# Local attention of a second layer on one core: token tiles on TensorE's row groups, keys with 32 tokens of the tile ahead, one score matmul for four heads

## The chip, the cores and the metric

The kernel runs on one core of a Trainium2 chip (trn2). The metric is the device time of one execution in microseconds (us); less is better. The core has five engines that run side by side and meet only at semaphores: TensorE (PE: matmuls, whose weight loads are listed apart as PEld), VectorE (DVE), ScalarE (ACT), GpSimd (POOL) and SyncE (SP), which issues transfers.

## The reference

Four blocks act on a hidden state x of 2 sequences of 1024 tokens with 128 features: window attention with 16 heads, a Fourier layer, an attention block (a global and a local attention), again the Fourier layer, a location-weighted layer, a mixture of experts, ReLU attention with its feed-forward part, and again experts. The change is in the local attention, which works on RMS-normed x:

```python
def local_gqa_attn(x, wq, wk, wv, wo):        # 16 heads of 8 features, 4 key heads
    q = split_heads(x @ wq, H)
    k = split_heads(x @ wk, KVH)
    v = split_heads(x @ wv, KVH)
    q, k = (rope(q, BASE_L), rope(k, BASE_L))
    q, k = (qk_norm(q), qk_norm(k))
    k, v = (repeat_kv(k), repeat_kv(v))
    i = jnp.arange(x.shape[1])
    diff = i[:, None] - i[None, :]
    mask = (diff >= 0) & (diff < WIN)         # WIN = 32
    return merge_heads(sdpa(q, k, v, mask)) @ wo
```

`rope` turns pairs of features by an angle that depends on the position, `qk_norm` divides each head by its root mean square, `sdpa` is softmax attention. A query sees itself and the 31 tokens ahead of it.

## The kernel before, in words

All 2048 tokens stay in SBUF, features on the 128 partitions and tokens along the free axis, in four chunks of 512 (`NC`), two for each sequence. Everything is float32 here, and a float32 matmul shows as two records in the trace (and two weight loads). Each engine runs a list of instructions of its own, in the order in which the functions of the same name stand in its block (`@block.tensor`, `@block.scalar` and so on); no planner moves them. They wait for one another at semaphores that only count up (`q["sc"]` counts score units in PSUM, `q["ex"]` exponentials done, and so on; `WAS` holds the counts of the attentions before). The local attention is the third attention (`AL`), in three parts.

**Heads** (`normed_heads(AL)`, on PE at L1794, DVE L1283, ACT L907, POOL L693). It works in eight units, queries and keys of each chunk by turns. PE projects a chunk twice (plain and rotated weights, 128 rows and columns, 512 tokens), DVE multiplies by the rope table and adds (L1303, L1304, L1307), ACT squares (L912), PE sums over each head ("var"), ACT takes logarithm and exponential (L919, L922), and POOL multiplies the factor in (L700). After every second unit PE projects the values of a chunk (8 records with the tokens as weights) and ACT copies them (L929). Queries and keys then have the four heads of a group on four row groups of 32 partitions. PE issues the var matmul of a unit behind the projection of the next one.

**Attention** (`local_attention` on PE at L1912, `local_soft` on ACT at L967, `local_attention` on DVE at L1348). It runs over eight passes (2 sequences x 4 groups of heads), each in two halves of four tiles of 128 tokens: 16 steps n. In a step PE computes scores (`scores(n)`, L1916) into PSUM banks 0 to 3, one bank for each head, in two pairs of heads: 32 matmuls of 32 rows x 64 columns of the array, each 64 keys against 96 queries. ACT exponentiates each pair (L986), DVE multiplies by the band mask (L1363), and two steps later PE multiplies by the values (`values(n)`, L1938) with matmuls of 64 rows x 32 columns: per tile 384 and 256 wide for the two halves of the keys, and 128 wide for the queries of the next tile. A pair of scores waits for the exponential of the same pair one step before. DVE masks the keys of the group for one pass ahead (`group_keys`, L1316), and ACT and DVE copy the sums out after every second pass (L974, L976, L1357).

**End** (`attention_end`). Denominators, reciprocals, the division, the output projection (64 records of 32x128 for two chunks), and the residual sums.

SP loads the rope tables: the local one (1 MB) when the heads of the global attention no longer need theirs (L660).

## Time and profile before

| | |
|---|---|
| median of 3 runs | 1024.35 us (1015.62, 1024.35, 1024.69) |
| the profiled execution | 1023.21 us, its span 1021.1 us |
| PE, DVE, ACT, POOL busy | 948.7, 535.3, 540.0, 147.7 us |
| mean granted clock of TensorE | 0.948 of full |
| projections of the local attention start | at 367.7 us of the span |
| its first score matmul | at 396.37 us |
| its last value matmuls | at 454.55 us |

The span is what the profiler saw between the first and the last instruction. The "granted clock" is TensorE's clock as a share of 2.4 GHz; it has two levels, 1.00 and 0.50 (1.2 GHz), and a mean between them is a mixture. Matmuls in different parts of the array overlap, so a busy PE doesn't mean a full array.

### The profile page before, as it was taken

Reading aid. Unit: us, or ns where it says so; the run is one execution under the profiler, and the core shown is the slowest. Engines: PE = TensorE matmul, PEld = TensorE weight load, DVE = VectorE, ACT = ScalarE, POOL = GpSimd, SP = SyncE. Lnnn points to the kernel's source line nnn. Section 1 sums busy time; section 2 is a strip of 40 time slices with the busy share of each in tenths; the row PEclk is TensorE's granted clock in tenths of the full one; section 3 lists DMA queues with packets and bytes.
Section 4 is the critical chain, followed back from the end, with each engine's and each line's share of the span. In section 5 each row is a group of like instructions: output and inputs, shape, how many; then the busy total and the mean of one; then the engine's idle time right before and its main releaser. Section 6 shows DMA issues by size and latency. Waiting matters only on the chain.

```text
span 1021.1 us, 22819 instructions
## 1 busy us (share of the span) xinstructions
PE 948.7 (93%) x9990; PEld 436.0 (43%) x9990; DVE 535.3 (52%) x870; ACT 540.0 (53%) x767; POOL 147.7 (14%) x164
## 2 busy tenths in 40 slices
PE   7698978999999988988998999989999999999998
PEld 4476733433333335754443444434333333444443
DVE  4576545523324375665565525555666666423554
ACT  6044535889999856443765531256455454445121
POOL 3001120501001003120010120000223322004000
PEclk9899989899999997589998799999999999899999
DMA  7644050100000000000000057100000000001651
GB/s 205 215 128 125 7 218 0 42 2 2 2 2 2 2 1 1 3 3 2 0 1 0 1 135 138 62 1 1 2 2 2 2 2 2 0 1 43 160 123 52
DMA packets 16763, 43.16 MB, mean 42 GB/s; under 512 B 4844, under 2 KB 5292, under 8 KB 15244
## 3 DMA queue, kind: packets, MB, share of 16 engines
q1 hardware_dynamic: 15692, 39.51, 14.5%
q10 hardware_dynamic: 972, 2.20, 0.7%
q8 instruction: 79, 1.29, 0.5%
q14 instruction: 20, 0.16, 0.1%
HBM read 36.91 MB, written 4.55 MB: 41 GB/s over the span
## 4 chain that ended last, share of the span: by engine, by line
PE 82%; ACT 8%; DVE 6%; issue 2%; DMA 1%; POOL 1%; ACTq 0%; SPq 0%; DVEq 0%; POOLq 0%
PE ps L1639 82%; ACT nrr L816 1%; ACT nrr L818 1%; ACT nsq L809 1%; DVE mxq L1258 1%; ACT work L897 1%; POOL work L677 1%; ACT nrr L826 0%; ACT nrr L823 0%; DMA stf<-scr_k 0%; DVE aux L1451 0%; DVE work L1307 0%; DMA x<-in_x 0%; PE ps L2072 0%; DVE work L1363 0%
## 5 line engine op out<-in xcount | busy, mean ns | idle before, releaser
L1639 PE MATMUL ps<-rq,stf 32*64 32x512 f32 (+4 forms) x4096 | 208.4, 465 | 3.3 <-ACT hz L1001 1.6
L1639 PE MATMUL ps<-work,vbuf 64*32 64x128 f32 (+6 forms) x2992 | 195.5, 421 | 2.4 <-DVE nsq L1357 2.2
L1639 PE MATMUL ps<-hz,wsb 128*128 128x512 f32 (+1 forms) x352 | 161.9, 624 | 5.0 <-ACT nsq L842 2.5
L957 ACT ACTIVATE work<-ps 128x1024 f32<-128x1024 f32 x144 | 139.5, 1021 | 14.3 <-PE ps L1639 10.4
L1639 PEld LDWEIGHTS ps<-rq,stf 32*64 32x64 f32 x4096 | 97.5, 147 | 110.2 <-issue 84.1
L1019 ACT ACTIVATE work<-ps 128x1024 f32<-128x1024 f32 x72 | 73.6, 1024 | 75.7 <-PE ps L1639 75.7
L1639 PEld LDWEIGHTS ps<-work,vbuf 64*32 64x32 f32 (+1 forms) x2992 | 62.9, 111 | 116.1 <-issue 64.4
L1639 PEld LDWEIGHTS ps<-hz,wsb 128*128 128x128 f32 (+1 forms) x352 | 62.8, 192 | 85.3 <-issue 73.2
L1341 DVE TENSOR_TENSOR work<-work,csb 128x1024 f32<-128x1024 f32 (+1 forms) x40 | 40.7, 1018 | 97.2 <-ACT work L957 96.8
L1065 ACT ACTIVATE work<-ps 128x512 f32<-128x512 f32 x48 | 28.7, 597 | 117.2 <-PE ps L1639 117.2
L1639 PE MATMUL ps<-work,wsb 128*128 128x512 f32 (+1 forms) x176 | 87.0, 603 | 2.7 <-DVE work L1553 2.7
L1402 DVE TENSOR_SCALAR work<-ps 128x1024 f32<-128x1024 f32 (+3 forms) x72 | 68.5, 952 | 24.2 <-PE ps L1639 24.2
L897 ACT ACTIVATE work<-ps 128x512 f32<-128x512 f32 x64 | 37.4, 598 | 65.3 <-PE ps L1639 65.3
L1550 DVE TENSOR_TENSOR work<-ps,work 128x512 f32<-128x512 f32 x48 | 33.2, 691 | 64.0 <-ACT work L1065 40.8
L1639 PE MATMUL ps<-bsb 128*64 128x512 bf16 x256 | 53.1, 398 | 13.8 <-DMA stf<-scr_k 7.4
L1639 PE MATMUL ps<-nsq,csb 128*128 128x512 f32 (+3 forms) x152 | 53.3, 530 | 10.8 <-DVE nrr L1253 3.0
L809 ACT ACTIVATE nsq<-ps 128x512 f32<-128x512 f32 x40 | 23.5, 588 | 62.4 <-PE ps L1639 62.4
L1258 DVE TENSOR_REDUCE mxq<-ps 128x4 f32<-128x512 f32 x64 | 42.8, 688 | 22.3 <-PE ps L1639 21.3
L1639 PEld LDWEIGHTS ps<-work,wsb 128*128 128x128 f32 (+1 forms) x176 | 31.9, 189 | 50.0 <-issue 34.3
L738 POOL TENSOR_TENSOR work<-work,csb 128x512 f32<-128x512 f32 (+1 forms) x40 | 36.4, 911 | 106.7 <-ACT work L1019 106.7
L719 POOL TENSOR_SCALAR aux<-nsq,csb 128x1024 f32<-128x1024 f32 x8 | 24.2, 3025 | 156.8 <-DVE nsq L1328 110.4
L1639 PE MATMUL ps<-x,csb 128*128 128x512 f32 x64 | 35.6, 663 | 6.3 <-DMA x<-in_x 4.8
(200 smaller groups left out, 1172.9 us busy)
## 6 DMA issues: line engine op xcount, KB each, us to landing
stf<-scr_w SPq DMA_DIRECT2D x32, 256.0 KB, 4.5
stf<-scr_w SPq DMA_DIRECT2D x64, 128.0 KB, 3.3
stf<-scr_q SPq DMA_DIRECT2D x12, 192.0 KB
wsb<-in_w SPq DMA_DIRECT2D x1, 2192.0 KB, 12.5
rq<-in_rq SPq DMA_DIRECT2D x2, 1024.0 KB, 9.9
stf<-scr_k SPq DMA_DIRECT2D x9, 204.0 KB
rq<-scr_k SPq DMA_DIRECT2D x6, 204.0 KB
hz<-scr_k SPq DMA_DIRECT2D x6, 204.0 KB
```

Source lines behind the costliest of these rows:

```text
L719: nc.gpsimd.tensor_scalar(nums[:, b * S:(b + 1) * S], half_out[0][:, b * S:(b + 1) * S], c_("part")[:, 0:1], None, ALU.mult).then_inc(q["s ...
L738: nc.gpsimd.tensor_tensor(cells, cells, c_("keep").unsqueeze(1).unsqueeze(1) .broadcast_to(list(cells.shape)), ALU.mult).then_inc(q["mk"], 1)
L809: nc.scalar.activation(nsq[:, c], bank(c), ACT.Square).then_inc(n_sq, 1)
L897: nc.scalar.activation(prob[:, st, hd], bank(n % 2), ACT.Exp, scale=SCALE).then_inc(q["ex"], 1)
L957: nc.scalar.activation(probs_of(n)[:, 2 * k:2 * k + 2].rearrange("p h s -> p (h s)"), two(slot(2 * n + k)), ACT.Exp, scale=SCALE).then_inc ...
L1019: nc.scalar.activation(probs_of(n)[:, 0:2].rearrange("p h s -> p (h s)"), two(slot(2 * n)), ACT.Relu, scale=SCALE).then_inc(q["ex"], 1)
L1065: nc.scalar.activation(moe[:, 0, f % 2], bank(f % 2), ACT.Silu).then_inc(m_sg, 1)
L1258: nc.vector.tensor_reduce(mxq[:, k % 2, 4 * u:4 * u + 4], bank(4 + m % 2).rearrange("p (t s) -> p t s", t=4), AX.X, ALU.max).then_inc(w_m, 1)
L1341: nc.vector.tensor_tensor(cells, cells, c_("keep").unsqueeze(1).unsqueeze(1) .broadcast_to(list(cells.shape)), ALU.mult).then_inc(q["mk"], 1)
L1402: ins = nc.vector.tensor_scalar(to[:, :, lo:hi], src[:, :, lo:hi], SCALE, 0.0, ALU.mult, ALU.max)
L1550: nc.vector.tensor_tensor(product, bank(2 + f % 2), moe[:, 0, f % 2], ALU.mult).then_inc(m_su, 1)
L1639: return nc.tensor.matmul(o, l, r, start=start, stop=stop, skip_group_check=True)
```

## The change

Row groups stand for token tiles in place of heads. A query unit is one of the four heads of every group for all 2048 tokens: eight matmuls with 32 columns of weights each, every one for one tile of each chunk, write to four column groups (`queries`). There are four such units. Keys are computed for two chunks per unit and in 2 units, for each tile of 128 tokens with the 32 tokens ahead of it (`KW` = 160 columns); so there are 6 units and not 8. The values of a chunk follow each of the four query units. The first scores wait for all four query units. A score matmul has a tile's keys against the queries of four heads at once: in each of two pairs of tiles, two blocks of 32x64 that are 384 and 256 wide for each tile, and then, for both tiles, a block of 32x32 that is 128 wide and has the 32 keys ahead. The value matmuls are the eight of before (64x32, 384 and 256 wide), and then four of 32x32 in place of 64x32, 128 wide, for the 32 keys ahead. The exponentials, the masks and the copies out keep their sizes. The masked keys of the four groups are made once for both sequences, in 4 instructions of 640 columns in place of 2 of 512 and 7 of 1024. The second rope load becomes 0.33 MB. `normed_heads`, `rotated_consumed` and `group_keys` stay for the other attentions.

```diff
+KW = P + WIN_L
+UNITS_L = 2 + G
...
+        rope_l = rq[:, 0:4 * KW].rearrange("p (k c s) -> p k c s", k=2, c=CB)
+        q_l = qd[:, 0:T].rearrange("p (h s) -> p h s", h=G)
+        k_l = stf[:, NG * T - NC * KW:NG * T].rearrange("p (c s) -> p c s", c=NC)
+        kz_l = stf[:, 0:NG * NC * KW].rearrange("p (g c s) -> p g c s", g=NG, c=NC)
...
+            return CB * KW if m < 2 else CH
...
-            rope_load(1)
+            sp.dma_start(rope_l, rope_k.rearrange("k p c s -> p k c s")).then_inc(s_rope, 16)
...
+            def local_heads():
+                was = WAS[AL]
+                for m in range(UNITS_L):
+                    rt_ = rope_t[:, m % 4]
+                    pool.wait_ge(q["r"], was["r"] + m + 1)
+                    if m < 2:
+                        nc.gpsimd.tensor_tensor(k_l[:, CB * m:CB * (m + 1)].rearrange("p c s -> p (c s)"),
+                                                rt_[:, 0, 0:CB * KW], rt_[:, 2, 0:CB * KW], ALU.mult).then_inc(q["kn"], 1)
+                    else:
+                        nc.gpsimd.tensor_tensor(q_l[:, m - 2], rt_[:, 0], rt_[:, 2], ALU.mult).then_inc(q["q"], 1)
...
+            def local_heads():
+                was = WAS[AL]
+                for m in range(UNITS_L + 1):
+                    if m < UNITS_L:
+                        rt_, w = rope_t[:, m % 4], unit_width(m)
+                        act.wait_ge(q["rot"], was["rot"] + m + 1)
+                        nc.scalar.activation(rt_[:, 1, 0:w], rt_[:, 0, 0:w], ACT.Square).then_inc(q["sq"], 1)
+                    if m:
+                        rt_, w = rope_t[:, (m - 1) % 4], unit_width(m - 1)
+                        act.wait_ge(q["var"], was["var"] + m)
+                        if m > 4:
+                            act.wait_ge(q["kn"], was["kn"] + m - 4)
+                        nc.scalar.activation(rt_[:, 2, 0:w], bank(pair(AL, m - 1))[:, 0:w], ACT.Ln, bias=eps[:, 1:2])\
+                            .then_inc(q["ln"], 1)
+                        act.wait_ge(q["ln"], was["ln"] + m)
+                        nc.scalar.activation(rt_[:, 2, 0:w], rt_[:, 2, 0:w], ACT.Exp, scale=-0.5).then_inc(q["r"], 1)
+                    if 2 <= m < 2 + NC:
+                        c = m - 2
+                        act.wait_ge(q["v"], was["v"] + c + 1)
+                        act.wait_ge(s_vz, 6)
+                        for g in range(NG):
...
-                    rotated_consumed(AL, n)
...
+            def local_group_keys(g):
+                if g == 0:
+                    dve.wait_ge(q["kn"], WAS[AL]["kn"] + 2)
+                nc.vector.tensor_scalar(kz_l[:, g].rearrange("p c s -> p (c s)"), k_l.rearrange("p c s -> p (c s)"),
+                                        group_mask(g), None, ALU.mult).then_inc(q["kz"], 1)
+            def local_heads():
+                was = WAS[AL]
+                dve.wait_ge(s_rope, 32)
+                for m in range(UNITS_L):
+                    rt_, w, o = rope_t[:, m % 4], unit_width(m), pair(AL, m)
+                    dve.wait_ge(q["mm"], was["mm"] + m + 1)
+                    if m >= 4:
+                        dve.wait_ge(q["kn"], was["kn"] + m - 3)
+                    for i in range(2):
+                        if m < 2:
+                            to, src = rt_[:, i, 0:w], bank(o + i)[:, 0:w]
+                            turn = rope_l[:, i].rearrange("p c s -> p (c s)")
+                        else:
+                            to = rt_[:, i].rearrange("p (b c s) -> p b c s", b=B, c=CB)
+                            src = bank(o + i).rearrange("p (b c s) -> p b c s", b=B, c=CB)
+                            turn = rope_l[:, i, :, WIN_L:KW].unsqueeze(1).broadcast_to([P, B, CB, P])
+                        ins = nc.vector.tensor_tensor(to, src, turn, ALU.mult)
+                    ins.then_inc(q["t"], 1)
+                    dve.wait_ge(q["t"], was["t"] + m + 1)
+                    nc.vector.tensor_tensor(rt_[:, 0, 0:w], rt_[:, 0, 0:w], rt_[:, 1, 0:w], ALU.add)\
+                        .then_inc(q["rot"], 1)
+                    if m >= 4:
+                        local_group_keys(m - 4)
...
-                    if n % 2 == 0 and n // 2 + 1 < len(PASSES):
-                        group_keys(AL, *PASSES[n // 2 + 1])
+                    if n < 2:
+                        local_group_keys(2 + n)
...
+                by_row_group = z.rearrange("p (c j s) -> p j c s", c=NC, j=4)
+                def keys(m):
+                    for i in range(2):
+                        for j in range(4):
+                            for k in range(CB):
+                                at = (CB * m + k) * CH + j * P - WIN_L
+                                skip = max(0, -at)
+                                ins = mm(bank(pair(AL, m) + i)[32 * j:32 * j + 32, k * KW + skip:(k + 1) * KW],
+                                         wk[i][:, 0:32], z[:, at + skip:at + KW])
+                    ins.then_inc(q["mm"], 1)
+                def queries(m):
+                    hd = m - 2
+                    for i in range(2):
+                        for j in range(4):
+                            ins = mm(bank(pair(AL, m) + i)[32 * j:32 * j + 32].rearrange("p (c s) -> p c s", c=NC),
+                                     wq[i][:, 32 * hd:32 * hd + 32], by_row_group[:, j])
+                    ins.then_inc(q["mm"], 1)
+                for m in range(UNITS_L + 1):
+                    if m < UNITS_L:
+                        pe.wait_ge(n_z, normed(n, 2 * m + 1 if m < 2 else NC - 1))
+                        if m >= 3:
+                            pe.wait_ge(q["ln"], was["ln"] + m - 2)
+                        (keys if m < 2 else queries)(m)
+                    if 2 <= m < 2 + NC:
+                        v = m - 2
+                        if v >= 2:
+                            pe.wait_ge(q["vf"], was["vf"] + v - 1)
+                        values_by_token(v, bank(6 + v % 2), w_("l_wv")).then_inc(q["v"], 1)
+                    if m:
+                        pe.wait_ge(q["sq"], was["sq"] + m)
+                        mm(bank(pair(AL, m - 1))[:, 0:unit_width(m - 1)], c_("head"),
+                           rope_t[:, (m - 1) % 4, 1, 0:unit_width(m - 1)]).then_inc(q["var"], 1)
...
+                    c = CB * b + n % 2
+                    if n == 0:
+                        pe.wait_ge(q["q"], was["q"] + G)
                     if n % 2 == 0:
-                        pe.wait_ge(q["kz"], was["kz"] + keys_of(AL, n // 2))
+                        pe.wait_ge(q["kz"], was["kz"] + (NG if b else g + 1))
                     for pair in range(2):
                         u = 2 * n + pair
-                        if u < 2:
-                            pe.wait_ge(q["ln"], was["ln"] + 2 * NC - 2 + u)
-                        else:
+                        if u >= 2:
                             pe.wait_ge(q["ex"], was["ex"] + u - 1)
-                        for j in range(4):
-                            k0 = b * S + (4 * (n % 2) + j) * P
-                            for half in range(2):
-                                at = k0 + HB * half
-                                for hd in (2 * pair, 2 * pair + 1):
-                                    rows = slice(32 * hd, 32 * hd + 32)
-                                    ins = mm(bank(hd)[HB * half:HB * (half + 1), j * W_L:(j + 1) * W_L],
-                                             kz[rows, g, at:at + HB], qd[rows, at:at + W_L])
+                        def block(j, lo, m, q0, w):
+                            rows = slice(32 * j, 32 * j + 32)
+                            o = bank(j)[lo:lo + m, 0:G * W_L].rearrange("p (h s) -> p h s", h=G)
+                            at = HB if m == WIN_L else 0
+                            first = 0 if m == WIN_L else WIN_L + lo
+                            return mm(o[:, :, at:at + w], kz_l[rows, g, c, first:first + m],
+                                      q_l[rows, :, c * P + q0:c * P + q0 + w])
+                        for j in (2 * pair, 2 * pair + 1):
+                            block(j, 0, HB, 0, W_L)
+                            block(j, HB, HB, HB, HB)
+                        for j in (2 * pair, 2 * pair + 1):
+                            if (n % 2, j) != (0, 0):
+                                ins = block(j, P - WIN_L, WIN_L, 0, WIN_L)
                         ins.then_inc(q["sc"], 1)
...
                     for j in range(4):
-                        for half in range(2):
-                            rows = slice(HB * half, HB * (half + 1))
-                            lo, w = HB * half, min(W_L, P - HB * half)
-                            mm(by_tile(4 + 2 * half + st, j)[:, :, lo:lo + w],
-                               vq[rows, KT * b + 4 * st + j, g // 2, g % 2], heads[rows, :, j * W_L:j * W_L + w],
-                               opens and (half, st, j) != (1, 1, 0), False)
-                    rows = slice(HB, P)
-                    if opens and st == 0:
-                        mm(by_tile(6, 0)[:, :, 0:WIN_L], qd[rows, T:T + WIN_L], heads[rows, :, 0:WIN_L], False, False)
-                    for j in range(4 - st):
-                        lo = j * W_L + HB
-                        ins = mm(by_tile(7 if j == 3 else 6 + st, (j + 1) % 4)[:, :, 0:WIN_L],
-                                 vq[rows, KT * b + 4 * st + j, g // 2, g % 2], heads[rows, :, lo:lo + WIN_L],
-                                 opens and j == 3, False)
+                        block(j, 0, HB, 4 * st + j, 0, 0, W_L, opens)
+                        ins = block(j, HB, HB, 4 * st + j, HB, 0, HB, opens)
+                    for j in range(4):
+                        if st + j:
+                            ins = block(j, P - WIN_L, WIN_L, 4 * st + j - 1, 0, HB, WIN_L, False)
+                        elif opens:
+                            ins = block(j, P - WIN_L, WIN_L, -1, 0, 0, WIN_L, False)
                     ins.then_inc(q["pv"], 1)
...
+        for c in range(CB):
+            at = np.maximum(P * (4 * c + row // 32) - WIN_L + np.arange(KW), 0)
+            k[0, row, c] = cos_l[at, d // 2]
+            k[1, row, c] = sign * sin_l[at, d // 2]
```

## Rows read from the trace of the kernel before

**Rows 1.** The page: busy time of each engine.

```profile
PE 948.7 (93%) x9990; PEld 436.0 (43%) x9990; DVE 535.3 (52%) x870; ACT 540.0 (53%) x767; POOL 147.7 (14%) x164
```

**Rows 2.** Stretches: us, busy (x) of PE, PEld, DVE, ACT, POOL; granted clock; DMA.

```profile
391.78:395.19 3.41, 1.93 (x11) 1.35 (x10) 2.62 (x4) 1.83 (x7) 1.27 (x1) 1.00 0.00 0
395.19:436.15 40.96, 39.80 (x920) 28.60 (x918) 23.07 (x18) 21.20 (x34) 5.37 (x3) 0.50 0.01 3
436.15:446.39 10.24, 8.10 (x325) 6.02 (x324) 9.02 (x8) 6.98 (x10) 0.00 (x0) 1.00 0.02 5
446.39:453.22 6.83, 6.41 (x132) 5.00 (x135) 3.31 (x3) 1.53 (x2) 4.28 (x1) 0.50 0.01 2
453.22:466.87 13.65, 6.79 (x152) 3.98 (x139) 9.21 (x18) 2.68 (x6) 2.36 (x3) 1.00 0.00 1
```

**Rows 3.** Timeline of the heads: start, us, engine, line, operands, count, [idle before].

```profile
369.70 0.75 DVE L1155 SCALAR_TENSOR_TENSOR hz<-hz,vsb,nrr 128x512 f32<-128x512 f32 x1 [0.58 <-ACT nrr L818]
...
380.20 1.88 PE L1639 MATMUL ps<-hz,wd 128*128 128x512 f32 x4
...
381.92 0.97 PE L1639 MATMUL ps<-wsb,hz 128*128 128x32 f32 x8
...
383.68 1.88 PE L1639 MATMUL ps<-hz,wd 128*128 128x512 f32 x4
...
386.25 1.88 PE L1639 MATMUL ps<-hz,wd 128*128 128x512 f32 x4
```

**Rows 4.** Timeline: the last heads and the first scores.

```profile
394.07 0.63 ACT L912 ACTIVATE work<-work 128x512 f32<-128x512 f32 x1 [1.58 <-DVE work L1307]
...
396.37 2.28 PE L1639 MATMUL ps<-rq,stf 32*64 32x96 f32 x64
...
397.19 0.63 ACT L922 ACTIVATE work<-work 128x512 f32<-128x512 f32 x1
...
397.90 1.26 POOL L700 TENSOR_TENSOR hz<-work 128x512 f32<-128x512 f32 x1 [0.62 <-ACT work L922]
```

**Rows 5.** Timeline: one step of the attention at clock 0.50.

```profile
413.47 2.28 PE L1639 MATMUL ps<-rq,stf 32*64 32x96 f32 x64
...
415.09 1.53 ACT L986 ACTIVATE work<-ps 128x768 f32<-128x768 f32 x2 [2.14 <-PE ps L1639]
...
416.65 1.76 DVE L1363 TENSOR_TENSOR work<-work,csb 128x1536 f32<-128x1536 f32 x1 [1.24 <-ACT work L986]
417.13 1.98 PEld L1639 LDWEIGHTS ps<-rq,stf 32*64 32x64 f32 x64 [0.38 <-issue]
```

**Rows 6.** Narrow cuts of the timeline: where one tile shape follows another.

```profile
415.37 0.38 PE L1639 MATMUL ps<-rq,stf 32*64 32x96 f32 x3
415.68 0.89 PE L1639 MATMUL ps<-work,vbuf 64*32 64x384 f32 x8
...
415.67 0.14 PEld L1639 LDWEIGHTS ps<-work,vbuf 64*32 64x32 f32 x3 [0.23 <-issue]
...
551.81 0.59 PE L1639 MATMUL ps<-work,stf 128*128 128x512 f32 x1
552.33 0.64 PE L1639 MATMUL ps<-stf,csb 128*32 128x512 f32 x4
```

**Rows 7.** Short stretches in one step's scores, columns as in rows 2.

```profile
414.14:414.30 0.16, 0.16 (x16) 0.16 (x16) 0.16 (x1) 0.00 (x0) 0.00 (x0) 0.50 0.00 0
...
415.44:415.60 0.16, 0.16 (x8) 0.01 (x2) 0.00 (x0) 0.16 (x1) 0.00 (x0) 0.50 0.00 0
```

**Rows 8.** Timeline: steps at clock 1.00, and the last value matmuls.

```profile
436.23 1.31 PE L1639 MATMUL ps<-rq,stf 32*64 32x96 f32 x64
...
437.47 0.88 PE L1639 MATMUL ps<-work,vbuf 64*32 64x384 f32 x22
...
438.28 1.36 PE L1639 MATMUL ps<-rq,stf 32*64 32x96 f32 x64
...
454.55 0.88 PE L1639 MATMUL ps<-work,vbuf 64*32 64x384 f32 x22
```

More of the change, by code:

```diff
@@ L585, in _ @@
                 constant_rows(k)
-            def rope_load(i):
-                sp.dma_start(rope, rope_q[i].rearrange("k p s -> p k s")).then_inc(s_rope, 16)
             def load_queries(k, i):
@@ L653, in _ @@
             sp.wait_ge(q["sc"], KT * (len(PASSES) - 1))
-            rope_load(0)
+            sp.dma_start(rope, rope_q.rearrange("k p s -> p k s")).then_inc(s_rope, 16)
             own = wsb[:, WAT["w_down"][0] + NPAIR * P:WAT["w_down"][1]]
@@ L933, in normed_heads @@
                         ins.then_inc(q["vf"], 1)
-                    if a == AG and 3 <= m < 3 + NC:
+                    if 3 <= m < 3 + NC:
                         hidden_factor(2, m - 3)
+            def local_heads():
[19 more added lines that the diff above has]
+                        for g in range(NG):
+                            ins = nc.scalar.activation(
+                                vq[:, 4 * c:4 * c + 4, g // 2, g % 2, columns_of(g, False)],
+                                bank(6 + c % 2)[:, 0:4 * KVH * D].rearrange("p (t g d) -> p t g d", t=4, g=NG)
+                                [:, :, g], ACT.Copy)
+                        ins.then_inc(q["vf"], 1)
             def rotated_consumed(a, n):
@@ L1807, in normed_heads @@
                             pe.wait_ge(n_z, normed(n, c))
-                        if a == AG and m < 3:
+                        if m < 3:
                             if m == 0:
@@ L1812, in normed_heads @@
                                 pe.wait_ge(n_z, first(n - 1, 2 * m - 1))
-                        if a == AL and m == 1:
-                            pe.wait_ge(n_ln, 4 * n + 2)
                         if m >= 3:
@@ L1822, in normed_heads @@
                         if v < 2:
-                            pe.wait_ge(n_z, first(n - 1, 2 + v) if a == AG else 4 * n + 3 + v)
+                            pe.wait_ge(n_z, first(n - 1, 2 + v))
                         else:
@@ L1829, in normed_heads, with local_heads @@
                         mm(bank(pair(a, m - 1)), c_("head"), rope_t[:, (m - 1) % 4, 1]).then_inc(q["var"], 1)
+            def local_heads():
+                was, n = WAS[AL], N_OF[AL]
+                wq, wk = (d_("l_wq"), d_("l_wqr")), (d_("l_wk"), d_("l_wkr"))
+                by_row_group = z.rearrange("p (c j s) -> p j c s", c=NC, j=4)
[30 more added lines that the diff above has]
+                           rope_t[:, (m - 1) % 4, 1, 0:unit_width(m - 1)]).then_inc(q["var"], 1)
             def relu_heads():
@@ L1941, in values @@
                     if n == 0:
-                        pe.wait_ge(q["ln"], was["ln"] + 2 * NC)
                         pe.wait_ge(q["vf"], was["vf"] + NC)
@@ L2255, in rope_tables, with turns @@
 def rope_tables():
-    q = np.zeros((2, 2, P, S), np.float32)
-    for n, base in enumerate((1000000.0, 10000.0)):
+    q = np.zeros((2, P, S), np.float32)
+    k = np.zeros((2, P, CB, KW), np.float32)
+    def turns(base, positions):
         inv = np.float32(1.0) / np.float32(base) ** (np.arange(0, D, 2, dtype=np.float32) / np.float32(D))
-        f = np.arange(S, dtype=np.float32)[:, None] * inv.astype(np.float32)[None, :]
-        cos, sin = np.cos(f).astype(np.float32), np.sin(f).astype(np.float32)
-        for row in range(P):
-            d = row % D
-            q[n, 0, row] = cos[:, d // 2]
-            q[n, 1, row] = (-1.0 if d % 2 == 0 else 1.0) * sin[:, d // 2]
-    return q, q[:, :, 0:1, 0:1].copy()
+        f = positions.astype(np.float32)[:, None] * inv.astype(np.float32)[None, :]
+        return np.cos(f).astype(np.float32), np.sin(f).astype(np.float32)
+    cos, sin = turns(1000000.0, np.arange(S))
+    cos_l, sin_l = turns(10000.0, np.arange(S))
+    for row in range(P):
+        d = row % D
+        sign = -1.0 if d % 2 == 0 else 1.0
+        q[0, row] = cos[:, d // 2]
+        q[1, row] = sign * sin[:, d // 2]
+        for c in range(CB):
+            at = np.maximum(P * (4 * c + row // 32) - WIN_L + np.arange(KW), 0)
+            k[0, row, c] = cos_l[at, d // 2]
+            k[1, row, c] = sign * sin_l[at, d // 2]
+    return q, k
 def window_bias():
```

31 lines of the change are left out of this document (16 added, 15 removed).

## The prediction

> **What bounds the kernel now.** I read the page first: PE is busy 93% of the span, with the other engines near half or below [rows 1], so the question is what PE does in this stage. Next the timeline of the stage. Its heads run from 367.7 us and its attention from 396.37 [rows 4] to the end of the last value matmuls, 454.55 + 0.88 = 455.4 [rows 8]. In a step at clock 0.50, PE goes from one score unit (413.47) to the next (417.13) in 3.66 us. ACT works 1.53 of it and DVE 1.76, and both sit idle before their work for 2.14 and 1.24 us [rows 5]. PE sets the pace, then. The table by stretches tells why it is slow: the clock is 0.50 for 41 us of the attention and again for 6.8 us, and 1.00 for 10.2 us between them, where a step takes 438.28 - 436.23 = 2.05 us [rows 2, 8].
>
> **How the array is shared.** Two 128x128 matmuls of 512 columns are four records in 381.92 - 380.20 = 1.72 us [rows 3]: 0.43 for a record, 0.84 ns for a column at clock 1.00, so 1.68 ns at 0.50. The 64 score records of 96 columns would need 10.3 us one after another at 0.50; they take 415.68 - 413.47 = 2.21 [rows 5, 6]. So parts of the array that don't overlap run at once. Value matmuls show it well: the busiest part (64 rows, 32 columns) has 256 + 128 columns twice, 768 x 1.68 = 1.29 us, and from the first of them to the next scores it is 417.13 - 415.68 = 1.45. About 0.15 is lost.
>
> Where is that lost? Around each change of shape. The last 32x64 records start at 415.37 and stream 0.16 us, to 415.53; the 64x32 ones start at 415.68 [rows 6]. And no part starts early. The second pair of scores, in another half of the rows, begins while the first runs (16 records and 16 weight loads under way at 414.14), and then finishes alone; yet in the last 0.16 us of scores the weight loads are at 0.01 us, although the first pair's rows are free and the values to come have nothing left to wait for: their mask ended at 416.65 - 2 x 3.66 + 1.76 = 411.1 [rows 5, 7]. With one shape there is overlap; with a new one PE waits until the whole array is empty, and 0.15 us more (0.14 to 0.15 at 0.50). At clock 1.00 a 128x128 record starts at 551.81 and streams 0.43, the 128x32 ones start at 552.33 [rows 6]: 0.09 us, for a change of columns alone.
>
> **Heads.** Eight units become six. A key unit costs each column group two blocks of 160 columns from two weights, twice over (two records): 1280 x 0.84 ns = 1.07 us. The first starts as before; the second needs all four chunks normalised, 369.70 + 0.75 = 370.45 [rows 3], and the first query unit follows its sums at about 373.0 (DVE's three operations and ACT's square at 5/8 of their size). From then on every query unit has the values of a chunk behind it. Such a unit took PE 383.68 - 380.20 = 3.48 us, one without values 386.25 - 383.68 = 2.57 [rows 3]. The eight query matmuls run in four column groups and cost the same 1.72 us, but they have another shape than values and sums: two changes, 0.2 us. So 3.68 us each: the last projection starts at 373.0 + 3 x 3.68 = 384.0 and ends at 385.8. DVE takes 2.2 us behind it, and from ACT's square to the end of POOL's product it was 397.90 + 1.26 - 394.07 = 5.1 us with the sum at 0.50 [rows 4]; at 1.00 I take 4.4. The scores can begin at 392.5, **3.9 us earlier** than 396.37. But PE has nothing to do from the last sum (389.7) on: before, the first scores didn't wait for the last product, now they do, 2.8 us.
>
> Edits with no price: DVE's key masks fall from 9 instructions to 4 and DVE had 1.24 us to spare in a step [rows 5]; if that cover went, it would still be less work. The rope load moves 0.33 MB in place of 1 MB, issued on SP at the same point, some 170 us before its use, with nothing of this stage queued behind it. The waits for consumed products on ACT go, since the first scores imply them. Exponentials, masks and copies keep their sizes.
>
> **Attention.** The work in columns is the same: a part of the array has 384 columns twice in a pair of scores before (4 x 96) and after (384, or 256 + 128). What changes is the shapes. A pair is now 32x64 and then 32x32, so a step has six changes of shape (four in and around scores, two with values) where it had two. What neither row shows is a change from 32x64 to 32x32. The nearest are the two of rows 6, one with a new number of rows and columns, one with a new number of columns alone, and both cost a gap; I take it that the array empties here too. At clock 0.50:
> - a pair: 768 x 1.68 = 1.29, a change 0.14, the small blocks 256 x 1.68 = 0.43, a change 0.14: 2.00 us; the second pair can't overlap any more: 4.0 us for the scores, against 2.21;
> - values: 1.29 + 0.14 + 0.43 + 0.14 = 2.0 us, against 1.45.
>
> So a step is 6.0 us, against 3.66. ACT (1.53) and DVE (1.76) are far below it. The stage is two steps of scores alone, 8.0, fourteen whole steps, 84.0, and at the end two value groups with the denominators between them, 2.0 + 1.9 + 2.0 = 5.9: 97.9 us. It ends at 392.5 + 97.9 = 490.4, **35.0 us later** than 455.4. The end section ran at clock 1.00 from 453.22 [rows 2] and would now begin at 0.50. It has 6.8 us of PE work, partly beside DVE; I add 2 us. Sum: 1023.21 + 35.0 + 2 = **1060 us**. The profiled execution is 1.1 us under the median, 1024.35, so nothing is corrected for that.
>
> The rule that speaks against the change is in the Trainium skill, "TensorEngine Tiling (Array Packing)", Key Properties: a change of tiling mode, not of the tile alone, drains TensorE, and 32x32 and 32x64 are two modes there. By that rule the steps are 6.0 us; by the row alone (a new shape in the same rows might run beside the others) they would be 2.9. The trace agrees for 32x64 to 64x32, and no row shows 32x64 to 32x32.
>
> **Which clock.** All this is at 0.50. Before, the clock fell at 395.19, behind a stretch in which PE was busy 1.93 of 3.41 us [rows 2]; now PE is idle for 2.8 us in the same place, and then begins with pairs that leave most of the array empty. It stayed at 0.50 for 41 us, though PE was busy for 39.80 of them, under a pattern that fills the array much better than the new one would. I see no reason for it to come back.
>
> **Rivals.**
> - *The clock comes back* (or never falls). Price of a step: 2 x (0.64 + 0.10 + 0.21 + 0.10) + 1.05 = 3.15 us. Stage: 4.2 + 14 x 3.15 + 3.1 = 51.4, end at 443.9, 11.5 us earlier: 1012 us. For it: 10.2 us at 1.00 in the middle of the old attention [rows 2]. Against: the 41 us. Between the two, with the clock at 1.00 for half of the time, about 1036. The Trainium skill's page "TensorE: Matmul & The Clock Gate", in "Why this matters for your kernels", says that a TensorE kept busy gets its full clock; by that rule the whole stage would be this rival's. The trace disagrees: 39.80 of 40.96 us busy, at 0.50.
> - *No drain: small and large blocks share the array* (the other side). If 32x32 can run beside 32x64 in other rows, both pairs overlap wholly, because there are 24 records in a step and not 64: 1.29 + 0.15 for the scores, 1.29 + 0.15 for the values, 2.9 us at 0.50. The array is then much fuller than before; I let the clock rise after three steps, and DVE would set the pace: 1.76, a quarter of 0.7 for adding, 0.2 for the rest, 2.15 us. Stage: 8.6 + 13 x 2.15 + 2.5 = 39.1, end at 431.6: 999 us. If the clock stayed low: 16 x 2.9 + 3, 1010 us. It decides at the first small block: whether the second pair starts beside it. For it: the rows (32) stay alike and only the columns change. Against: rows 6, where the rows stay alike too and the gap is there.
>
> **How the numbers follow.** Forecast (drain, low clock) 0.74; drain with the clock back for a part 0.04, for all 0.05; no drain 0.15; something that I don't see, which leaves the time where it is, 0.02. The forecast's own range: without the gap, only the waiting for an empty array, a step is 5.15, 1047 us; with 0.24 a change (half as much again, near the idle 0.38 of the weight loads [rows 5] less their 0.14), about 1070. So 1046 to 1070 beside 1060. To leave out no more than 2 in 10 the range must also take in the clock's cases, down to 1010: 1010 to 1070. About 1% (10 us) is what a measurement can tell from no change, since the runs before differ by 9 us. Slower by over 1%: 0.74 and most of 0.04, 0.77. Faster by over 1%: 0.05 and 0.15, 0.20. Within: 0.03.
>
> **What would show it.** In the trace after: the first scores at 392 to 393 us behind an idle of about 2.8; PE's starts within a step in six groups, and none of the second pair's before the first pair's small blocks have streamed; 6.0 us from step to step, with ACT and DVE idle for over 4 of it; a granted clock of 0.50 from some 392 to 490. I am wrong if small-block and second-pair weight loads overlap the first pair (then look for 999), or if the clock is 1.00 in the attention (1012).

## The result, and the profile after

The changed kernel takes 1058.58 us (median of 4 runs, 1055.23 to 1065.71), the kernel before, timed beside it, 1023.97 (4 runs, 1015.62 to 1024.69): a ratio of 1.0382, 95% interval 1.0335 to 1.0428. It is slower by 35 us, and the forecast was 1060. Of the runs below, one (1128.84 us, at a mean granted clock of 0.812 where the other three of its kernel have 0.931 to 0.935) is left out of its kernel's ratio.

The profiled execution took 1055.23 us, 3.4 under its median, with a span of 1053.4. On the page the line of busy times, to be read against [rows 1], and the granted clock in 40 slices:

```profile
PE 979.3 (93%) x9426; PEld 411.5 (39%) x9426; DVE 525.5 (50%) x859; ACT 537.4 (51%) x761; POOL 143.1 (14%) x162
...
PEclk9899989999999995555799899999999999999999
```

The trace has 564 fewer matmul records (a matmul is two), and PE is busy for longer. The slices at 5 are the attention. The table by stretches, cut where the clock changes (columns as in [rows 2]):

```profile
394.70:395.89 1.19, 1.19 (x14) 0.40 (x18) 0.00 (x0) 0.00 (x0) 0.00 (x0) 1.00 0.00 0
395.89:491.46 95.57, 95.57 (x726) 21.74 (x726) 32.33 (x22) 29.22 (x38) 5.69 (x2) 0.50 0.00 1
491.46:494.88 3.42, 1.49 (x32) 0.49 (x32) 0.97 (x2) 1.89 (x4) 2.00 (x2) 1.00 0.00 0
494.88:511.94 17.06, 12.36 (x162) 9.14 (x155) 8.95 (x18) 0.80 (x2) 0.36 (x2) 0.50 0.00 1
```

The attention lies at 0.50 from 1.2 us behind its first score to its last value matmuls, without one free moment on PE, while DVE and ACT work a third of the time. "Busy" is not "full" here: PE counts as busy for all of these 95.57 us, although most of the matmuls are 32x64, an eighth of the array each.

The weight loads of one step show the order best, since each load stands just ahead of its matmul (timeline, PEld alone, and ACT's and DVE's rows of the same step; compare [rows 5]):

```profile
414.15 0.30 PEld L1716 LDWEIGHTS ps<-rq,stf 32*64 32x64 f32 x8 [0.38 <-issue]
...
415.63 0.18 PEld L1716 LDWEIGHTS ps<-rq,stf 32*32 32x32 f32 x2 [1.18 <-issue]
416.19 0.30 PEld L1716 LDWEIGHTS ps<-rq,stf 32*64 32x64 f32 x8 [0.38 <-issue]
416.30 0.81 ACT L1032 ACTIVATE work<-ps 128x768 f32<-128x768 f32 x1 [3.25 <-PE ps L1716]
417.67 0.18 PEld L1716 LDWEIGHTS ps<-rq,stf 32*32 32x32 f32 x4 [1.18 <-issue]
418.24 0.22 PEld L1716 LDWEIGHTS ps<-work,vbuf 64*32 64x32 f32 x16 [0.39 <-issue]
...
418.36 0.81 ACT L1032 ACTIVATE work<-ps 128x768 f32<-128x768 f32 x1 [1.25 <-PE ps L1716]
419.20 1.76 DVE L1440 TENSOR_TENSOR work<-work,csb 128x1536 f32<-128x1536 f32 x1 [4.36 <-ACT work L1032]
419.70 0.19 PEld L1716 LDWEIGHTS ps<-work,vbuf 32*32 32x32 f32 x6 [1.23 <-issue]
420.27 0.30 PEld L1716 LDWEIGHTS ps<-rq,stf 32*64 32x64 f32 x8 [0.38 <-issue]
```

Six groups, each beginning 1.18 to 1.23 or 0.38 us after the last load of the one before: wide, small, wide, small, wide values, small values, and then the next step, 6.12 us after the first. Within a group the two tiles (in values, the four) run side by side, but no group begins beside the one before it. Where [rows 5] has ACT idle for 2.14 us, it now waits 3.25 and 1.25, and DVE waits 4.36 in place of 1.24.

### The profile page after: what moved, and what is told of

Read it like the earlier page. It is cut to its first block, busy times and chain, and to the rows that moved or that the text cites. A ratio compares the mean times of both kernels' runs of the same rounds, so it can differ in the third digit from the quotient of the medians.

```text
span 1053.4 us, 21660 instructions
## 1 busy us (share of the span) xinstructions
PE 979.3 (93%) x9426; PEld 411.5 (39%) x9426; DVE 525.5 (50%) x859; ACT 537.4 (51%) x761; POOL 143.1 (14%) x162
## 4 chain that ended last, share of the span: by engine, by line
PE 83%; ACT 8%; DVE 5%; issue 2%; DMA 1%; SPq 1%; ACTq 0%; POOL 0%; DVEq 0%; POOLq 0%
PE ps L1716 83%; ACT nrr L836 1%; ACT nrr L838 1%; ACT nsq L829 1%; DVE mxq L1304 1%; ACT work L917 1%; ACT nrr L846 0%; DMA stf<-aux 0%; ACT nrr L843 0%; DMA stf<-scr_k 0%; DVE aux L1528 0%; PE ps L2188 0%; DMA x<-in_x 0%; ACT nsq L862 0%; ACT work L1004 0%
## 5 line engine op out<-in xcount | busy, mean ns | idle before, releaser
L1716 PE MATMUL ps<-rq,stf 32*64 32x512 f32 (+4 forms) x3440 | 240.5, 518 | 5.1 <-issue 3.1
L1716 PE MATMUL ps<-work,vbuf 64*32 64x128 f32 (+6 forms) x2992 | 204.6, 427 | 0.8 <-issue 0.6
L1716 PE MATMUL ps<-hz,wsb 128*128 128x512 f32 (+1 forms) x352 | 158.0, 604 | 5.0 <-ACT nsq L862 2.5
L1004 ACT ACTIVATE work<-ps 128x1024 f32<-128x1024 f32 x144 | 139.4, 1022 | 13.5 <-PE ps L1716 9.2
L1716 PEld LDWEIGHTS ps<-rq,stf 32*64 32x64 f32 (+1 forms) x3440 | 84.4, 136 | 155.8 <-issue 128.6
L1065 ACT ACTIVATE work<-ps 128x1024 f32<-128x1024 f32 x72 | 73.7, 1025 | 75.6 <-PE ps L1716 75.6
L1716 PEld LDWEIGHTS ps<-work,vbuf 64*32 64x32 f32 (+1 forms) x2992 | 57.6, 110 | 127.5 <-issue 80.2
L1440 DVE TENSOR_TENSOR work<-work,csb 128x1536 f32<-128x1536 f32 x16 | 28.1, 1758 | 64.0 <-ACT work L1032 64.0
L1032 ACT ACTIVATE work<-ps 128x768 f32<-128x768 f32 x32 | 26.0, 811 | 60.3 <-PE ps L1716 60.3
```

What stands on the lines that cost most here:

```text
L1004: nc.scalar.activation(probs_of(n)[:, 2 * k:2 * k + 2].rearrange("p h s -> p (h s)"), two(slot(2 * n + k)), ACT.Exp, scale=SCALE).then_inc ...
L1065: nc.scalar.activation(probs_of(n)[:, 0:2].rearrange("p h s -> p (h s)"), two(slot(2 * n)), ACT.Relu, scale=SCALE).then_inc(q["ex"], 1)
L1440: nc.vector.tensor_tensor(cells, cells, band, ALU.mult).then_inc(q["mk"], 1)
L1716: return nc.tensor.matmul(o, l, r, start=start, stop=stop, skip_group_check=True)
```

## Experiments

Theory 1 is the prediction's: every change of tile shape empties the array and costs a gap besides. Theory 2: no emptying, the matmuls are only held up by their order in PE's queue (a block that waits for its part of the array holds up those behind it). Theory 3: long, strided matmuls (four heads at once) are slow in themselves. The first four kernels were timed together against 1019.62 us of the kernel before (19 runs), the next four against 1018.61 (13 runs), the last two against 1017.88 (19 runs).

### One shape in scores, one in values

```diff
-        kz_l = stf[:, 0:NG * NC * KW].rearrange(...)
+        kz_l = stf[:, WIN_L:WIN_L + NG * NC * KW].rearrange(...)
 ...
-                                ins = block(j, P - WIN_L, WIN_L, 0, WIN_L)        # scores
+                                ins = block(j, HB, HB, 0, WIN_L)
 ...
-                            ins = block(j, P - WIN_L, WIN_L, 4 * st + j - 1, 0, HB, WIN_L, False)   # values
+                            ins = block(j, HB, HB, 4 * st + j - 1, 0, HB, WIN_L, False)
```

The block of the 32 keys ahead becomes 64 keys wide; it takes in the 32 columns that lie ahead of those keys in memory (the masked keys are moved up by 32 columns to make room), and the 32 extra rows are zeroed by the mask. Streamed columns stay the same.

> The blocks for the 32 keys ahead get the shape of their neighbours: 64 columns in the scores, 64 rows in the values, with the same widths and the same results. Theory 1 (each change of shape empties the array): two changes a step are left, the pairs overlap, a step is 1.29 + 0.14 + 1.29 + 0.14 = 2.9 us at clock 0.50 against 6.12; 1058 - 16 x 3.2 = 1007 us, and some 999 if the clock comes back. Theory 2 (no drain: PE takes matmuls in order, and a block that waits for its columns holds up what stands behind it): the ahead block still waits for the 256-wide one, 0.86 us, and the second pair behind it: about 3.8 us a step, 1021 us. Theory 3 (the wide matmuls with a moving operand of four strided pieces are slow in themselves): no change, 1058.

Measured: 1006.71 us (1002.19 to 1008.24, 4 runs), ratio 0.9865 (0.982 to 0.991): 52 us off the changed kernel, by a change of shape and what the clock made of it. Theory 1 said 1007, theory 2 1021, theory 3 1058. Its timeline (PE; two steps, the first begun at clock 0.50, the second at 1.00, which came at 406.15):

```profile
403.95 1.66 PE L1716 MATMUL ps<-rq,stf 32*64 32x384 f32 x24
405.54 1.14 PE L1716 MATMUL ps<-work,vbuf 64*32 64x384 f32 x24
406.62 1.44 PE L1716 MATMUL ps<-rq,stf 32*64 32x384 f32 x22
```

All 24 score records of both pairs lie in one stretch of 1.6 us, at 0.50: the pairs share the array. The same records took 4.1 us in the changed kernel.

Then one half of the edit at a time. Scores only:

> Only the score blocks for the keys ahead are made 32x64, the value blocks stay 32x32. Theory 1: the scores fall from 4.08 to 1.43 us, the values stay 2.03: 3.5 us a step at 0.50, 1058 - 16 x 2.65 = 1016 us; about 1001 if the clock comes back. Theory 2: 2.2 + 2.03 = 4.2 a step, 1028. Theory 3: 1058.

Measured: 1025.06 us (1019.59 to 1027.99, 10 runs), ratio 1.0048 (1.002 to 1.0076). Weight loads at 0.50, and from the same view the one row of PE that waits:

```profile
410.62 1.20 PEld L1716 LDWEIGHTS ps<-rq,stf 32*64 32x64 f32 x24 [0.38 <-ACT work L1032]
412.14 0.26 PEld L1716 LDWEIGHTS ps<-work,vbuf 64*32 64x32 f32 x16 [0.33 <-DVE work L1440]
413.62 0.20 PEld L1716 LDWEIGHTS ps<-work,vbuf 32*32 32x32 f32 x8 [1.22 <-issue]
414.20 0.34 PEld L1716 LDWEIGHTS ps<-rq,stf 32*64 32x64 f32 x16 [0.38 <-issue]
...
416.33 1.53 PE L1716 MATMUL ps<-work,vbuf 64*32 64x384 f32 x16 [0.54 <-DVE nsq L1434]
```

A step is 3.58 us: scores 1.52 (they were 4.09), values 2.06 as they were. The time missed the expected one by 9 us, although this step did not: 1053.4 - 1023.9 = 29.5 us of span went, where 16 x 2.65 = 42 were expected. The stage gave 34.7 (table below): not every step is 3.58, since three of the 14 whole ones take 4.16, with PE waiting for DVE's copy of the sums (416.33 above), and the two steps of scores alone had less than 2.65 each to lose. The stages behind it, at their own clock, took 5.5 back (1023.9 - 457.70 against 1053.4 - 492.73).

Values only:

> Only the value blocks for the keys ahead are made 64x32, the score blocks stay 32x32. Theory 1: the values fall from 2.03 to 1.45 us, so a step is 5.54 and the clock stays 0.50: 1058 - 9 = 1049 us. Theory 2: the value blocks there wait for the longer 384-wide ones no more, same 1049. Theory 3: 1058.

Measured: 1048.64 us (1045.1 to 1050.47, and one run of 1128.84), ratio 1.0272 (1.0218 to 1.0326).

```profile
411.59 0.30 PEld L1716 LDWEIGHTS ps<-rq,stf 32*64 32x64 f32 x8 [0.38 <-issue]
...
415.68 0.22 PEld L1716 LDWEIGHTS ps<-work,vbuf 64*32 64x32 f32 x16 [0.38 <-issue]
...
417.14 0.30 PEld L1716 LDWEIGHTS ps<-rq,stf 32*64 32x64 f32 x8 [0.39 <-issue]
```

A step is 5.55 us: scores still 4.09, values 1.46 in place of 2.03. The two halves are worth 2.54 and 0.57 us of the 6.12, which leaves 3.01. In the kernel with both, scores at 0.50 take 1.59 us (403.95 to 405.54); with 1.46 for the values that is 3.05.

### The same shapes, grouped or interleaved

```diff
                         for j in (2 * pair, 2 * pair + 1):
                             block(j, 0, HB, 0, W_L)
                             block(j, HB, HB, HB, HB)
+                    for pair in range(2):
                         for j in (2 * pair, 2 * pair + 1):
```

Both pairs' wide blocks first, then both pairs' small ones: four changes of shape in a step for six.

> All blocks keep their shapes; the small blocks of both score pairs come together behind the large ones of both pairs, so a step has four changes of shape and not six. Theory 1: scores 1.33 + 0.14 + 0.43 + 0.14 = 2.04 us against 4.08, a step 4.1 at 0.50: 1058 - 33 = 1025 us. Theory 2: 1.33 + 0.43, without gaps, 3.8 a step: 1021. Theory 3: 1058.

Measured: 1022.15 us (1016.87 to 1027.77, 10 runs), ratio 1.0028 (0.999 to 1.0067). The time alone lies between theory 1 (1025) and theory 2 (1021); the step tells them apart.

```profile
408.10 0.33 PEld L1716 LDWEIGHTS ps<-rq,stf 32*64 32x64 f32 x16 [0.38 <-issue]
409.61 0.19 PEld L1716 LDWEIGHTS ps<-rq,stf 32*32 32x32 f32 x6 [1.18 <-issue]
410.18 0.22 PEld L1716 LDWEIGHTS ps<-work,vbuf 64*32 64x32 f32 x16 [0.38 <-issue]
411.63 0.19 PEld L1716 LDWEIGHTS ps<-work,vbuf 32*32 32x32 f32 x6 [1.23 <-issue]
412.20 0.33 PEld L1716 LDWEIGHTS ps<-rq,stf 32*64 32x64 f32 x16 [0.38 <-ACT work L1032]
```

A step at 0.50 is 4.10 us, as theory 1 said; theory 2 said 3.8. Not one matmul differs from the changed kernel; the order alone, with the full clock that part of the stage then got (0.73 on average), gives 36 us. That ends theory 3. Then the other way, the small block straight behind each tile's wide ones:

```diff
                             block(j, 0, HB, 0, W_L)
-                            block(j, HB, HB, HB, HB)
-                        for j in (2 * pair, 2 * pair + 1):
+                            ins = block(j, HB, HB, HB, HB)
                             if (n % 2, j) != (0, 0):
```

> The changed kernel with the small block of a tile placed straight behind the tile's two wide ones, so that a pair of scores goes 32x64, 32x32, 32x64, 32x32 in place of 32x64, 32x32: same matmuls, same columns, four more changes of shape in a step. Theory 1 (each change empties the array and costs 0.13 to 0.15 us at clock 0.50): the tiles of a pair can no longer share the array, a pair is 4.0 us, a step about 10.1 us in place of 6.12, 16 steps are 64 us more: 1122 us. Theory 2 (no emptying, only the order in the queue): the second tile's wide blocks stream in other rows beside the first tile's, the step stays at 6 us: 1058 us. Theory 3 (long strided matmuls are slow in themselves): 1058 us too.

Measured: 1108.57 us (1106.52 to 1112.45, 4 runs), ratio 1.0862 (1.0811 to 1.0914). Theories 2 and 3 said 1058.

```profile
417.10 0.29 PEld L1716 LDWEIGHTS ps<-rq,stf 32*64 32x64 f32 x4 [0.38 <-issue]
418.57 0.18 PEld L1716 LDWEIGHTS ps<-rq,stf 32*32 32x32 f32 x2 [1.18 <-issue]
419.13 0.29 PEld L1716 LDWEIGHTS ps<-rq,stf 32*64 32x64 f32 x4 [0.38 <-issue]
...
427.24 0.30 PEld L1716 LDWEIGHTS ps<-rq,stf 32*64 32x64 f32 x8 [0.38 <-issue]
...
435.36 0.29 PEld L1716 LDWEIGHTS ps<-rq,stf 32*64 32x64 f32 x4 [0.38 <-issue]
```

A tile is 2.03 us, as a pair was: tile by tile, although the tiles sit in different rows. An odd step is 10.14 us (417.10 to 427.24), as expected; an even one only 8.12 (to 435.36). The expectation had forgotten that tile 0 of an even step has no keys ahead in scores, so that tiles 0 and 1 still go together. 8 x 4.02 + 8 x 2.00 = 48 us; the stage grew by 49.0.

### All scores 32x32

```diff
+                            for part in range(lo, lo + m, 32):
+                                ins = mm(o[:, :, at:at + w], kz_l[rows, g, c, first:first + 32],
 ...
-                            ins = block(j, P - WIN_L, WIN_L, 4 * st + j - 1, 0, HB, WIN_L, False)   # values
+                            ins = block(j, HB, HB, 4 * st + j - 1, 0, HB, WIN_L, False)
```

> The other way to one shape: every score block cut into 32x32 ones (twice the wide ones' number, same columns in each part of the array), and the 32 keys ahead made 64x32 in the values. Theory 1: the price was the change of shape, not the small shape, so this goes as with all blocks wide: 1000 to 1010 us, with the two pairs of scores beginning within 0.5 us of each other. If the 32x32 shape itself were slow (for instance its loads of weights, which are now 40 in a step for the scores): 1040 us or more.

Measured: 1009.36 us (1004.37 to 1013.45, 4 runs), ratio 0.9884 (0.983 to 0.9938). Theory 1 said 1000 to 1010. The small shape is not slow either; only the alternation is.

### The attention in eight kernels

One stretch of each trace, from the first score to the end of the last value matmul (columns as in [rows 2], one kernel a fence, in this order: before, changed, one shape each, scores only, values only, grouped, interleaved, all 32x32):

```profile
396.37:455.43 59.06, 55.33 (x1417) 40.59 (x1416) 35.79 (x27) 29.70 (x46) 9.29 (x4) 0.61 0.01 3
```

```profile
394.68:492.73 98.05, 98.05 (x760) 22.49 (x760) 32.33 (x22) 30.02 (x40) 5.69 (x2) 0.51 0.00 1
```

```profile
395.58:442.26 46.68, 39.73 (x760) 24.90 (x760) 31.89 (x22) 27.53 (x40) 8.68 (x2) 0.82 0.01 2
```

```profile
394.31:457.70 63.39, 60.57 (x760) 22.84 (x760) 32.07 (x22) 28.24 (x40) 5.69 (x2) 0.50 0.01 2
```

```profile
392.31:481.99 89.68, 89.68 (x760) 27.02 (x760) 32.35 (x22) 29.88 (x40) 5.68 (x2) 0.51 0.00 1
```

```profile
392.42:454.06 61.64, 56.07 (x760) 15.33 (x760) 33.10 (x22) 28.04 (x40) 5.69 (x2) 0.73 0.01 2
```

```profile
394.77:541.81 147.04, 147.03 (x760) 33.38 (x760) 32.34 (x22) 30.03 (x40) 5.69 (x2) 0.50 0.00 1
```

```profile
398.50:447.22 48.72, 44.37 (x1016) 24.15 (x1016) 32.70 (x22) 28.47 (x40) 7.13 (x2) 0.86 0.01 3
```

Six of them have 760 records with the same streamed columns, and they take from 46.7 to 147.0 us. Of those at 0.50 throughout, or but for 1.2 us, three changes of shape in a step take 63.4 us, five 89.7, six 98.1, and ten or eight 147.0. Grouped (four), all 32x32 and one shape each (two), in which PE is not always busy, also get part of the stage at 1.00. Their times are therefore not only the price of the changes of shape; for that the steps at 0.50 are the ones to compare.

### What the clock does

Three more matmuls of 512 columns, or five, in PE's idle time ahead of the first scores:

```diff
+                for k in range(3):
+                    mm(bank(3), c_("head"), ch(z, k % NC))
```

> The changed kernel with three more 128x512 matmuls, whose result nobody reads, in the 3.1 us in which PE waits for the last product before the first scores; they take 2.6 us of it. Question: does the clock fall because of this idle time? If it does, and the shapes don't matter, the clock stays at 1.00 and a step is 3.15 us: about 1012 us. If the attention's own pattern (half of the array empty, an emptied array six times in a step) holds it down, the fall comes a few us later and the time is 1055 to 1060 us. I expect the second.

Measured: 1053.24 us over 10 runs, but these make two heaps: four runs at 1010.81 to 1017.95 with a mean clock of 0.967 to 0.974, six at 1050.71 to 1061.41 with 0.925 to 0.932, so that no single ratio describes them. The lower four alone are at 0.9951 of the kernel before (0.9913 to 0.9988). The profiled run is of the upper heap. The four runs of the changed kernel had all been in the upper heap.

> The changed kernel with five extra 128x512 matmuls ahead of its first scores in place of three (nobody reads their result; 4.3 us in an idle time of 3.1, so the scores begin up to 1.7 us later). With three, the runs fell into two heaps: 1010.8 to 1018.0 us (4 of 10) and 1050.7 to 1061.4 (6 of 10), at mean clocks of 0.967 to 0.974 and 0.925 to 0.932. If the two heaps are one and the same pattern at either clock, more work ahead of it should put more runs, perhaps all, into the lower heap, at 1012 to 1017 us; the profile then shows a step of 3.2 to 3.4 us at clock 1.00, with the shape changes all there. If the low clock comes from the attention's own pattern, most runs stay at 1055 to 1062.

Measured: 1056.56 us, again two heaps: four of 10 runs at 1015.92 to 1019.75 (clock 0.972 to 0.973), six at 1055.01 to 1060.64 (0.925 to 0.930); the lower four are at 0.9992 of the kernel before (0.9954 to 1.0029). More work ahead did not shift the odds. No run of a lower heap was profiled, but the mean clocks fit a stage at full clock: 98 us at 0.50 in place of 1.00 are 0.047 of a span of 1053 us, and the heaps are some 0.045 apart. So neither expected outcome covers both heaps: the pattern does not always pull the clock down, and the idle time is not all that decides. And in the lower heaps the changed kernel, with all its changes of shape, is about as fast as the kernel before: the 35 us were lost by the emptied array and the low clock together. The profile, of the upper heap, shows how it goes wrong (timeline, then two stretches):

```profile
391.66 4.46 PE L1716 MATMUL ps<-hz,csb 128*128 128x512 f32 x10
...
396.05 0.21 PEld L1716 LDWEIGHTS ps<-rq,stf 32*64 32x64 f32 x8 [0.76 <-issue]
...
397.18 0.21 PEld L1716 LDWEIGHTS ps<-rq,stf 32*64 32x64 f32 x8 [0.20 <-issue]
```

```profile
396.05:401.93 5.88, 5.88 (x61) 1.92 (x64) 2.61 (x3) 3.36 (x5) 0.00 (x0) 1.00 0.00 0
401.93:408.00 6.07, 6.07 (x52) 1.39 (x48) 3.59 (x3) 1.72 (x3) 0.00 (x0) 0.50 0.01 3
```

PE was busy without a gap from 391.66 on and had full clock for 5.88 us of the attention; the clock fell in the middle of it all the same. A pair took 1.13 us at 1.00 (396.05 to 397.18), against 2.04 at 0.50.

The traces without filling show the other half. In all seven of them (the changed kernel, one shape each, scores only, values only, grouped, interleaved, all 32x32) PE is idle for 3.08 to 3.09 us ahead of the first score, and the clock falls between 1.2 us before that score and 1.2 us behind it. In three it has fallen before any score ran: at 391.83 for values only (first score 392.31), 391.93 for grouped (392.42), 393.62 for interleaved (394.77). There the clock fell in the idle time itself; in the kernel with five matmuls it fell with no idle time behind it since 391.66. So either can bring the fall. Last, the kernel with one shape each and three such matmuls ahead:

> The kernel with all blocks wide (one shape in the scores, one in the values) with the same three matmuls ahead of the first scores. There the clock was 0.50 from 396 to 406 us and a cold step took 3.2 us against 2.0 to 2.6. If the idle time made it fall, the clock now stays at 1.00 and about 4 us are gained on that kernel's 1007: 1002 to 1004 us. If the clock falls all the same, 1007 us, or 1 us more for the matmuls.

Measured: 1004.89 us (1003.6 to 1010.45, 4 runs), ratio 0.9861 (0.9804 to 0.9917). In its trace the clock was 1.00 from 371.77 to 440.04 and the stage took 41.8 us in place of 46.7, but the medians differ by 1.8 us and the intervals overlap: a gain over the kernel without the filling is not shown.

The kernel before with two such matmuls ahead of its last sum of squares:

> The kernel before with two extra 128x512 matmuls ahead of the last sum of squares of the heads, in the 1.5 us in which PE waits there (nobody reads their result; 0.24 us longer). If the idle time made the clock fall at 395.19, the clock stays at 1.00, some 11 steps of 3.66 us become 2.05 us, and the time falls by up to 17 us: 1002 to 1008 us. If the 96-column pattern is what brings the low clock, no change: 1018 to 1024 us. Either way the kernel with all blocks wide (1007 us) should be compared with this number, not with the kernel before alone, to tell what its shapes are worth at the same clock.

Measured: 1017.45 us (1015.59 to 1023.02, 10 runs), ratio 0.9986 (0.9957 to 1.0014): no change.

```profile
395.00:400.00 5.00, 2.25 (x108) 1.87 (x92) 2.41 (x3) 4.04 (x10) 2.05 (x2) 1.00 0.01 3
400.00:410.00 10.00, 9.93 (x248) 7.49 (x256) 5.86 (x5) 3.94 (x6) 0.00 (x0) 0.53 0.01 3
```

The clock was kept through the heads, but at full clock PE outran ACT at once (2.25 us busy of 5.00) and the clock fell at 400.52 in place of 395.19. So the kernel before gains nothing from this gap being filled, and the 1.35% of the kernel with one shape each (0.982 to 0.991, against 0.9957 to 1.0014 here) is not that of a filled gap.

## Why the prediction was right

**Place and mechanism.** The step that carried it, that a change from 32x64 to 32x32 empties the array, was taken from rows of other shapes [rows 6, 7]. It is now shown in three ways: by the loads of the changed kernel, by grouping (a step of 4.10 us for 6.12, 1022 us), and by interleaving (10.14 us, 1109 us). The rule of the Trainium skill that stood beside it ("TensorEngine Tiling (Array Packing)", Key Properties: a change of mode drains TensorE) agrees with the trace here as well, for a change in the number of columns alone. The rival without drain (999 us) fell at its own deciding point: the second pair waits for the first pair's small blocks. What this rival would have given is close to what one shape per phase gave, 1007.

**Sizes.**
- A pair: 2.04 us against 2.00 forecast. Two narrow cuts of the timeline, as in [rows 6], show a pair's last wide records and its small ones:

```profile
414.85 1.20 PE L1716 MATMUL ps<-rq,stf 32*64 32x384 f32 x3
...
415.64 1.47 PE L1716 MATMUL ps<-rq,stf 32*32 32x128 f32 x6
```

  With the prediction's 1.68 ns for a column, the last 384 have streamed at 414.85 + 0.65 = 415.50 and the small blocks' 256 at 415.64 + 0.43 = 416.07, and the next pair's loads come at 416.19: 0.13 us on average for a change, forecast 0.14. The rest is in the wide part, 1.34 against 1.29. Values took 2.03 against 2.0, a step 6.12 against 6.0.
- The stage: 98.05 us against 97.9. Fourteen steps took 85.7, not 84.0; the two steps of scores alone 7.2, not 8.0, since the clock was still 1.00 for 1.2 us; the end 5.1, not 5.9, since it came back at 491.46.
- The heads: the first row below answers to the last DVE row of the norm in [rows 3]; all before the stage is 371.28 - 369.70 = 1.58 us late in this execution. The first score follows at 394.68, 3.3 us earlier on that count than 396.37 [rows 4], where 3.9 were forecast. A query unit took PE 3.80 us, not 3.68 (the query matmuls 1.86, not 1.72). PE's idle ahead of the scores was 3.09 us, not 2.8: it waits for POOL's last product.

```profile
371.28 0.75 DVE L1201 SCALAR_TENSOR_TENSOR hz<-hz,vsb,nrr 128x512 f32<-128x512 f32 x1 [0.58 <-ACT nrr L838]
...
378.13 1.92 PE L1716 MATMUL ps<-hz,wd 128*32 128x512 f32 x16
...
381.94 1.92 PE L1716 MATMUL ps<-hz,wd 128*32 128x512 f32 x16
...
393.32 1.26 POOL L721 TENSOR_TENSOR rq<-work 128x512 f32<-128x512 f32 x1 [0.32 <-ACT work L972]
...
394.68 2.23 PE L1716 MATMUL ps<-rq,stf 32*64 32x384 f32 x16 [3.09 <-issue]
```

- The end: from the last values to the next norm's first matmuls 17.94 us (492.73 to 510.67) against 14.98 before (455.43 to 470.41): 3.0 more where 2 were forecast. The clock was 0.50 from 494.88 to 511.94, as the reason given has it; that all 3.0 come from it is not shown.

**The sum.** The last values end 37.30 us later, and with the end section it is 40.26. Of this 1.58 lay ahead of the stage; 7.9 came back behind it, in stages that the change doesn't touch, where the clock was 0.97 in place of 0.93 (510.67 to 633.47 took 122.80 us, the same work before 127.26) and, in the 341 us after that, 0.99 in place of 0.98 (3.5 us). So 32.3 us of span in these two executions, 34.6 between the medians, 37 forecast. That the forecast came out within 2 us was in part luck: the 7.9 that came back was in no term of the sum. Against it stood the 1.6 ahead of the stage, 0.7 more in heads and stage (37.30 - 1.58 against 35.0), 1.0 more in the end section, and a profiled execution that lies 3.4 under its median. The bound of 1070 called a gap of 0.24 us half as much again as 0.14; it is 70% more, which changes nothing here.

**The clock.** Forecast at 0.50 from 392 to 490; it was from 395.89 to 491.46. The reason given for the fall, PE's idle time and then a thin pattern, is borne out: the clock fell in the idle time in three traces, and without it in one. That the clock would not come back held in all four runs and in the trace. With the idle filled, 8 of 20 runs were in the lower heap, 1011 to 1020 us, which is where the rival "the clock comes back" stood (1012 us, chance 0.05 for all of the stage), so its price looks right. Whether the filling opened that heap is not shown: at odds of 8 in 20, four runs without filling would all be in the upper heap about once in eight times. So the 0.05 may have been too low, and part of the forecast's 0.74 lucky. What a filled gap would do was not considered. The rule from "TensorE: Matmul & The Clock Gate" in the Trainium skill, that a busy TensorE gets full clock, the trace contradicts more strongly than before, with busy as the profile counts it: 95.57 us out of 95.57, at 0.50.

**Still open:** what decides between the two heaps, and why the scores-only kernel stayed at 0.50 for 68 us while the one with one shape each left it after 10 (406.15). No run here tells that apart.

## What to carry to other kernels

Count the changes of tile shape in PE's order, rows and columns both, before counting matmuls or columns: in these traces, matmuls in different parts of the array ran side by side only when they had one shape. A block that is padded to its neighbour's shape, at the same streamed columns, cost nothing here, and so did one that was moved to stand with its like; padding turned +3.8% into -1.35%. And look at the granted clock of the stage before pricing anything in it: the same pair of scores took 2.04 us at 0.50 and 1.13 at 1.00.

## What was not expected of the hardware

- Two sorts of execution of one and the same kernel, 40 us apart, with mean clocks of 0.97 and 0.93, on a single core.
- PE without a gap at full clock, and the clock falls within the attention: at 401.93, with PE busy since 391.66; and at 394.79 in the kernel with three extra matmuls, 3.1 us behind its first score and an idle of 0.51.
